# GpSimd adds the probabilities of both heads of a step in one operation; the waits on these adds count steps instead of heads

## What is computed

```python
qkv = einsum('bchw,oc->bohw', x, w_qkv)              # q, k, v: 8 heads x 64 x 1024
sim = einsum('bhdi,bhdj->bhij', q * 64**-0.5, k)
attn = softmax(sim, axis=-1)
out = einsum('bhij,bhdj->bhid', attn, v)
y = einsum('bchw,oc->bohw', out, w_out) + b_out
y = y * rsqrt(mean(y * y, axis=channels) + 64**-0.5) * rms_scale
return y + x
```

## Time and profile before

| | |
|---|---|
| runs (us) | 4138.54, 4138.56, 4134.59; median 4138.54 |
| profiled execution | 4134.53, of which the span from first to last instruction is 4132.7 |
| TensorE clock granted, mean | 0.992 |
| one image in the steady part | 253.2 us |
| GpSimd: adds of probabilities | 1792, each 128x512 |

### The profile page before, as it was taken

How to read it: one execution, slowest core, us unless ns; L and a number is a source line. 1 busy time by engine, 2 the same in 40 slices (tenths; PEclk the granted TensorE clock), 3 DMA queues, 4 the chain that set the end, 5 groups by cost and what they waited for, 6 DMA issues and landing times.

```text
span 4132.7 us, 53813 instructions
## 1 busy us (share of the span) xinstructions
PE 4025.3 (97%) x18624; PEld 2410.5 (58%) x18624; DVE 2982.8 (72%) x3196; ACT 2274.2 (55%) x3969; POOL 2862.8 (69%) x2204
## 2 busy tenths in 40 slices
PE   7999999999999999999999999999999999999996
PEld 5665565655556565565655655556555555655553
DVE  5677777777777777677777777777777777777765
ACT  4556555555555555555565555655556555555553
POOL 4667676676776767767676776767667666676766
PEclk9999999999999999999999999999999999999997
DMA  3111111111111101111011011111111111111100
GB/s 144 41 52 42 52 41 62 51 52 41 62 52 41 60 33 67 46 42 72 31 62 52 34 69 33 60 52 41 62 52 43 50 49 63 43 51 41 64 19 31
DMA packets 71277, 212.25 MB, mean 51 GB/s; under 512 B 8152, under 2 KB 8280, under 8 KB 58208
## 3 DMA queue, kind: packets, MB, share of 16 engines
q1 hardware_dynamic: 71008, 208.80, 14.1%
HBM read 168.92 MB, written 39.85 MB: 51 GB/s over the span
## 4 chain that ended last, share of the span: by engine, by line
PE 63%; issue 14%; POOL 9%; DVE 8%; ACT 6%; DMA 0%; POOLq 0%; ACTq 0%; SPq 0%; DVEq 0%
PE pv L611 13%; PE aux L454 13%; PE score L596 9%; PE aux L514 7%; PE score L598 7%; PE aux L487 7%; PE aux L574 5%; POOL prob_sum L1017 5%; ACT probs L680 2%; DVE maxima L856 2%; POOL prob_sum L1013 1%; DVE inv_sum L913 1%; DVE rms_b L899 1%; DVE y_sb L926 1%; POOL x_lo L294 1%
## 5 line engine op out<-in xcount | busy, mean ns | idle before, releaser
L1017 POOL TENSOR_TENSOR prob_sum<-prob_sum,probs 128x512 f32<-128x512 f32 x1536 | 1985.3, 1318 | 402.0 <-ACT probs L680 401.1
L680 ACT ACTIVATE probs<-score 128x512 f32<-128x512 f32 x2048 | 1110.6, 595 | 928.0 <-PE score L598 920.5
L856 DVE TENSOR_REDUCE maxima<-aux 128x1 fp32r<-128x1024 f32 (+1 forms) x1024 | 1032.4, 1018 | 783.5 <-PE aux L574 727.9
L611 PE MATMUL pv<-probs,v_sb 128*64 128x512 f32 x4096 | 993.5, 606 | 0.0
L596 PE MATMUL score<-q_hl,k_hh 128*128 128x512 f32 x2048 | 881.4, 430 | 10.0 <-ACT probs L680 8.3
L598 PE MATMUL score<-q_hm,k_l 72*128 72x512 f32 x2048 | 816.5, 399 | 0.0
L1013 POOL TENSOR_TENSOR prob_sum<-probs 128x512 f32<-128x512 f32 x256 | 345.0, 1370 | 655.6 <-ACT probs L680 655.6
L454 PE MATMUL aux<-x_hi,w_ring 128*128 128x512 f32 x2048 | 657.9, 402 | 16.8 <-POOL x_lo L294 11.2
L596 PEld LDWEIGHTS score<-q_hl,k_hh 128*128 128x128 f32 x2048 | 387.4, 189 | 277.7 <-issue 185.2
L611 PEld LDWEIGHTS pv<-probs,v_sb 128*64 128x64 f32 x4096 | 248.4, 136 | 483.5 <-issue 431.2
L454 PEld LDWEIGHTS aux<-x_hi,w_ring 128*128 128x128 f32 x2048 | 365.5, 189 | 143.5 <-issue 68.9
(11 more groups left out here) (76 smaller groups left out, 4762.4 us busy)
## 6 DMA issues: line engine op xcount, KB each, us to landing
w_ring<-w_split SPq DMA_DIRECT2D x93, 1024.0 KB, 4.8
x_stage<-x SPq DMA_DIRECT2D x128, 256.0 KB, 4.5
resid<-x SPq DMA_DIRECT2D x128, 256.0 KB, 5.7
out<-resid SPq DMA_DIRECT2D x128, 256.0 KB, 2.0
w_split<-w_ring SPq DMA_DIRECT2D x3, 1024.0 KB, 12.1
w_split<-y_sb SPq DMA_DIRECT2D x3, 1024.0 KB, 3.9
y_sb<-wqkv SPq DMA_DIRECT2D x4, 512.0 KB, 8.2
probs<-wqkv SPq DMA_DIRECT2D x2, 512.0 KB, 6.8
```

The lines of the kernel that those rows point to most:

```text
L611: pe.matmul(pv[half][e * D:(e + 1) * D, :], v_sb[:, pair // 2, j, (pair % 2) * P + e * D:(pair % 2) * P + (e + 1) * D], probs[:, j % 4, e, ...
L680: act.activation(probs[:, j % 4, e, :], score[e][:], ACT.Exp, scale=SOFT).then_inc(prob_ready, 1)
L856: dve.tensor_reduce(maxima[:, n:n + 1], bank(k, banks), AX_X, ALU.max).then_inc(aux_free[k], 1)
L1017: pool.tensor_tensor(prob_sum[:, e, :], prob_sum[:, e, :], probs[:, j % 4, e, :], ALU.add).then_inc(prob_added, 1)
```

## The change

`add_probs` issues one operation for a step where it issued two: it waits until both heads' probabilities are there and adds 128x1024 elements at once (`prob_sum[:]` is both heads, `probs[:, j % 4]` likewise). `prob_added` then rises by 7 in a slot where it rose by 14, and the two readers of it, `sums` on TensorE and `exponentials` on ScalarE, count accordingly. What each of them waits for is otherwise the same: `sums` the last add of the slot, the exponential of step `j` the add that frees its place in the ring.

```diff
-                pe.wait_ge(prob_added, 14 * done)
+                pe.wait_ge(prob_added, 7 * done)
...
-                        base = (body.b * SLOTS + slot) * 14
-                        added = base + (2 * max(j - 5, 0) + e + 1 if j >= 4 else 2 * (j + 3) + e + 1 - 14)
+
+                        added = (body.b * SLOTS + slot) * 7 + (max(j - 5, 0) + 1 if j >= 4 else j + 4 - 7)
                         act.wait_ge(prob_added, added)
...
-                base = (body.b * SLOTS + slot) * 14
-                for e in range(2):
-                    n = body.b * 128 + slot * 16 + 2 * j + e
-                    pool.wait_ge(prob_ready, n + 1)
-                    if j == 1:
-                        if e == 0 and not (body.first and slot == 0):
-                            pool.wait_ge(sums_ready, SLOTS * body.b + slot)
-                        pool.tensor_tensor(prob_sum[:, e, :], probs[:, 0, e, :], probs[:, 1, e, :],
-                                           ALU.add).then_inc(prob_added, 1)
-                    else:
-                        pool.wait_ge(prob_added, base + 2 * (j - 2) + e + 1)
-                        pool.tensor_tensor(prob_sum[:, e, :], prob_sum[:, e, :], probs[:, j % 4, e, :],
-                                           ALU.add).then_inc(prob_added, 1)
+
+                pool.wait_ge(prob_ready, body.b * 128 + slot * 16 + 2 * j + 2)
+                if j == 1:
+                    if not (body.first and slot == 0):
+                        pool.wait_ge(sums_ready, SLOTS * body.b + slot)
+                    pool.tensor_tensor(prob_sum[:], probs[:, 0], probs[:, 1], ALU.add).then_inc(prob_added, 1)
+                else:
+                    pool.wait_ge(prob_added, (body.b * SLOTS + slot) * 7 + j - 1)
+                    pool.tensor_tensor(prob_sum[:], prob_sum[:], probs[:, j % 4], ALU.add).then_inc(prob_added, 1)
```

## The result

The changed kernel takes 4244.2 us (median of four runs, 4243.1 to 4246.5), the kernel before 4137.4 (4134.6 to 4138.6): a ratio of 1.026, with a 95% interval of 1.025 to 1.028. It is 107 us slower, 7.2 us for each image of the steady part. 4231 was forecast, in a range of 4150 to 4285.

The account below looks back on a forecast made before the run. TensorE, busy 97% of the span, was taken as the bound, GpSimd's saving as worth nothing. Delays behind longer turns summed to 6.4 us an image, 96 us over 15, on 4134.5: 4231 us, range 4150 to 4285.

Parts of the forecast that it names:

- the turns: VectorE operations with two SBUF inputs and GpSimd instructions each wait for the other's end; waits up to 2.39 us, not 1.3.
- part two: The add waits for both heads and ends 0.4 us later; bounds 0 to 51 us, taken as 0.
- part three: VectorE waits up to 2.39 us behind long adds, so TensorE's banks come late: 6.4 us an image, 96 us.
- Slot 6: TensorE's line 574 late behind the subtractions of line 849 by 1.35 us, later behind line 884 by about 0.3.
- Slot 2: Scalings of line 926 wait for long adds and delay TensorE; 3.0 us taken, between 1.0 and 5.1.
- The 1.0 before line 574: Slot 2: first line 926 waits out the add, so line 849's subtractions free the bank about 1.0 us late.
- the 1.9 that was left open: Slot 2: second line 926 or the next add gets the turn; 0 or 1.9 us for line 454's projection.
- The last two scalings: Slot 2: last two line 926, before maxima for which TensorE already waits 0.47 us; from 0 to 2.2 us.
- Slot 0: Line 905 1.6 us later; the reductions behind it end late for TensorE's transpose: 0.85 us.
- Slot 5: Two line 294 behind a long add delay the maxima reduction that frees line 487's bank: 0.7 us.
- Slot 1: Four line 926, but TensorE waits for `o_lo` anyway and lateness mostly comes out of that wait: 0.2 us.
- Slots 3, 4, 7: Line 905 at most 1.6 us later, output adds behind it have slack: 0, up to 0.5 us each.

## Why the prediction was right, and where not

The bound. TensorE set the time before and after, and GpSimd's 161 us less (120 to 220 forecast) brought nothing. With the turns gone, long and short adds take the same time.

The turns. The reading of line 905's spread held: its longest is one add, 1.31 us with short adds and 2.36 with long ones, and taking the two-input operations away took the loss away. The Trainium skill's rule for the shared ports ("SBUF — State Buffer", "SBUF: two separate sides") thus holds here for an instruction of 2.39 us as it did for one of 1.3.

The start of the add (part two). This step failed as it was put: nothing was taken for it on the ground that its readers have slack, and alone it costs 28 us. The readers do have slack; the step overlooked that an add that starts later also meets VectorE operations otherwise. In the sum it wasn't missed, since part three reckoned with the late starts. How the 107 us divide into late start and length can't be told by subtraction, because a longer add also makes dearer each collision that the late start brings.

Slot 6: 1.35 + 0.3 were forecast, 1.29 measured. The first wait was 1.19, so that under 0.1 is left for the second: line 905 found GpSimd idle, as forecast, and TensorE, late by then, had given VectorE some time.

Slot 2: 3.0 forecast, 3.84 measured, and right only in part. The 1.0 before line 574 came out at 1.01. The second scaling lost its turn to the add, the 1.9 that was left open (a wait of 1.70). The last two scalings cost nothing; the slack of a late TensorE took them, and with them the waits of 0.25 and 0.47 us that stood in this slot before. So the waits add 2.0 us, where 3.0 were forecast. In place of the rest stands a term that the prediction didn't have: the clock, 1.8 us an image on average (1.4 to 1.7 in eleven images, 2.6 in four). One error hides half of the other.

Slot 0: 0.85 forecast, 0.87 measured, with one step wrong. The waiting matmul isn't the transpose but the projection ahead of it, for whose bank the first of the two reductions is enough; that the number agrees so closely is partly luck. Slot 5: 0.7 and 0.91, of which 0.6 is line 487's longer wait and the rest mainly a wait of 0.26 us that wasn't in the sum, of scores (line 596) for an exponential. Slot 1: 0.2 and 0.27, the net of a new wait of 0.63 before line 487 and a wait for `o_lo` that fell from 0.79 to 0.50, as reasoned. Slots 3, 4, 7: 0 and 0.03 together.

The sum was 6.4 an image where it is 7.2, and 15 x 7.2 = 108 is the loss. Of the 7.2 some 5.4 are what the prediction reckoned with, waits behind the turns, and 1.8 the clock: the total came out closer than its terms.

## What to carry to other kernels

Fusing two operations of an engine that isn't the bound saved nothing here, and it can cost a great deal if another engine has to wait for the end of the fused one. Look for lines whose least and most are far apart though their size is fixed: the most tells what they take turns with, and a longer partner makes it longer. What such a wait costs is decided by its place, so put operations that take turns behind those that release something, and check what then stands behind them, on the engine that reads their result too: moved scalings without the residual add that reads them gave back less than half of what was hoped for.

## What the runs showed of the hardware

The clock was not expected. TensorE's granted clock fell to near half after two waits of 1.01 and 1.70 us with four short matmuls and one step's scores between them, and the matmuls of the projection behind them took 0.63 us in place of 0.39. After 0.93 and 1.35 us it fell in 7 of 15 images; with the second wait 0.4 us longer, slot 2 was long in all 15. After single waits of 1.19 us (slot 6) the slot's time shows no such term, and in two images of the kernel whose adds start late TensorE waited 1.44 us before line 574 in slot 2 at full clock. In or behind the wait of 1.58 us before line 514, which began 9 us behind the one of 1.0, it fell in 12 of 15 images. Why it falls in some images and not in others with the same waits was not tested.

A memset on VectorE took 485 ns in each of 128 executions of 128x512, and 61 ns in each of 128 of 128x3, beside the same adds for which line 905 waited up to 2.36 us.
